# Dynamic depthwise convolution block: two taps of the upper channels made by ScalarE and GpSimd, 50 side columns, rings of x without copied rows

## Chip, core and metric

One of the eight cores of a Trainium2 chip. The metric is the device time of one execution in microseconds (us), as the median of the runs shown.

## What is computed

Two layers, each `x = x + f(gn(x))`, on x of 16 images x 128 channels x 128 x 128, in float32. `gn` is a group normalization over groups of four channels.

```python
def _L0_conv_ref(x, w_in, b_in, kg_w1, kg_b1, kg_w2, kg_b2, w_out, b_out):
    xh = _conv1x1(x, w_in, b_in)                      # 128 -> 256 channels
    pooled = jnp.mean(xh, axis=(2, 3))
    hcx = jax.nn.relu(pooled @ kg_w1.T + kg_b1)
    kernels = (hcx @ kg_w2.T + kg_b2).reshape(b, c, K, K)   # a 3x3 kernel per image and channel
    y = jax.lax.conv_general_dilated(x_r, k_r, window_strides=(1, 1), padding=((1, 1), (1, 1)),
                                     feature_group_count=b * c, ...)   # depthwise
    y = y * jnp.tanh(jax.nn.softplus(y))              # Mish
    return _conv1x1(y, w_out, b_out)                  # 256 -> 128 channels
...
x = x + _L0_conv_ref(_gn(x), ...)
x = x + _L1_conv_ref(_gn(x), ...)     # FFT over channels, two 1x1 products, inverse FFT, real part, ReLU
```

The second layer is linear in front of its ReLU, so that it is one product with a 128 x 128 matrix made at the start.

## The kernel before

**Strips and slots.** An image is 16 strips of 8 rows (1024 positions a channel), the batch N = 256 strips. Channels lie on the 128 partitions. Each engine runs its own `slot(n)` once for every strip n; semaphores alone tie the engines together. In slot n the depthwise convolution of strip n is made, x of strip n+2 is cast and multiplied by w_in, the output product of strip n-1 is made, and the second layer of strip n-19 (LAG1), since it needs the statistics of a whole image.

**Who makes the depthwise convolution.** The lower 128 of the 256 channels of the first product are made by TensorE: taps and w_in are multiplied into nine 128 x 128 matrices per image (`tap_matrices` on VectorE, `taps_high` on ScalarE, `taps_low` on GpSimd), and `conv(n, t, taps)` runs, for each half strip t and each of the nine taps, three half-precision matmuls (high part of weights and x, high and low, low and high) of 4 rows x 88 columns into psA. The leftmost SIDE = 40 columns of these channels don't go there: `product_side` makes the first product for 41 columns, ScalarE puts it into `side` (`evacuate_side`), makes tap 0 from it into PSUM (`first_tap_side`), and VectorE adds taps 1 to 8 (`side_tap`, into accS). The upper 128 channels are made wholly on this way: `product_b` into psB, one bank for both halves, `evacuate(n, t)` into `xh`, tap 0 by `first_tap_b` into accB, taps 1 to 8 by VectorE's `tap`. So VectorE makes eight taps of 1024 elements and eight of 320 per strip.

**Behind it.** ScalarE applies Mish to the three results (`mish_conv`, `mish_side`, `mish_taps`). `product_out(n, t)` multiplies by w_out into psO, again one bank for both halves, and VectorE's `residual(n, t)` adds it to x in X and sums it. `layer1` multiplies x of strip n-19 into psL, `relu` on ScalarE puts it into zt, `add` on GpSimd adds it to x, and SyncE stores.

**Rings.** `hi` and `lo` hold the high and low half-precision parts of x, four strips and two more rows (RING + 2) of 130 columns: the rows at either end of the ring are copies of the rows at its other end, or zero at the border of an image, made by ScalarE's `edge_row` and in GpSimd's `cast`. `xh` and `side` are rings of the same kind. X holds 24 strips of x; SyncE loads strip n+4 in slot n once strip n-20 is stored.

**What sets the order.** Every engine works through its slot as written, and a wait holds back all that stands behind it. Besides the strip's work, the slots of an image carry small work at strips 1 and 2 (statistics of layer 1 for the image before) and 11 to 15 (statistics, kernels and tap matrices of the next image). In strips 2 and 12 `stats_rstd` takes a logarithm and an exponential, each with its own activation table, and the next Mish loads its own again.

## Time and profile before

| | us |
|---|---|
| median of 3 runs | 4215.98 (4215.41 to 4216.52) |
| the profiled execution | 4214.95 |
| its span | 4213.2 |
| TensorE matmuls busy | 4105.5 (97%) |
| VectorE busy | 3971.9 (94%) |
| ScalarE busy | 3080.4 (73%) |
| GpSimd busy | 1345.4 (32%) |
| granted TensorE clock, mean | 0.996 of 2.4 GHz |

The span is the time from the first to the last instruction of the profiled execution. Busy time is what an engine's instructions cover; matmuls and ScalarE's and VectorE's instructions overlap their neighbours a little, so that their spacing, from start to start, is shorter than their duration. A number in square brackets in a timeline is the idle time of the engine before the row, and the arrow names what ended it. Over 4000 of the 4213 us are the 256 slots; some 69 us stand before the first tap of VectorE, and some 50 us behind the last slot, for the second layer of the last image.

### The profile page before, as it was taken

The page shows a single profiled execution, that of the slowest core. Times are in us where ns is not written, and L with a number is a line of the kernel's source. Part 1 is how long each engine was busy: PE and PEld are TensorE (multiplying, and loading weights), DVE is VectorE, ACT ScalarE, POOL GpSimd, SP SyncE. Part 2 cuts the span into 40 slices and gives each one's busy share as a digit, 9 for nine tenths or more (in the row PEclk, how much of TensorE's full clock was granted, in tenths as well). Part 3 has the DMA queues.
Part 4 walks back from the last instruction along what each step waited for, and adds up shares of the span by engine and source line. Part 5 has one row for each costly group of instructions (what it writes and reads, how often), then busy time and mean ns, then how long its engine had stood idle before and what let it go on. Part 6 is the DMA issues. An engine that isn't in the chain of part 4 may idle for free.

```text
span 4213.2 us, 61339 instructions
## 1 busy us (share of the span) xinstructions
PE 4105.5 (97%) x21484; PEld 2214.4 (53%) x21484; DVE 3971.9 (94%) x5228; ACT 3080.4 (73%) x5443; POOL 1345.4 (32%) x1428
## 2 busy tenths in 40 slices
PE   5999999999999999999999999999999999999998
PEld 3455555555555555555555555555555555555553
DVE  6999999999999999999999999999999999999996
ACT  4767777777777777777777777777777777776654
POOL 1112333333333333333333323333233333333332
PEclk9999999999999999999999999999999999999999
DMA  3112223222222322222222222222222222222112
GB/s 137 51 61 76 101 95 105 94 103 96 100 101 95 105 96 100 100 96 101 97 99 100 96 102 99 100 101 96 100 99 97 101 99 103 96 100 76 61 65 115
DMA packets 111264, 401.59 MB, mean 95 GB/s; under 512 B 13232, under 2 KB 14320, under 8 KB 110704
## 3 DMA queue, kind: packets, MB, share of 16 engines
q1 hardware_dynamic: 110960, 397.67, 27.1%
q8 instruction: 174, 2.85, 0.3%
q14 instruction: 130, 1.06, 0.1%
HBM read 263.40 MB, written 134.22 MB: 94 GB/s over the span
## 4 chain that ended last, share of the span: by engine, by line
PE 82%; DVE 11%; ACT 3%; issue 2%; POOL 1%; SPq 0%; DMA 0%; ACTq 0%; DVEq 0%; POOLq 0%
PE psBO L704 18%; PE psA L657 15%; PE psA L658 14%; PE psA L659 14%; PE psL L713 9%; DVE accB L895 6%; DVE accS L906 3%; PE psBO L682 2%; PE psBO L684 2%; PE psBO L683 2%; PE psA L667 1%; DVE X L916 1%; POOL lo L1071 1%; PE psBO L693 1%; PE psBO L695 1%
## 5 line engine op out<-in xcount | busy, mean ns | idle before, releaser
L895 DVE SCALAR_TENSOR_TENSOR accB<-xh,vectors,accB 128x1024 f32<-128x1024 f32 x2048 | 2633.2, 1286 | 67.1 <-ACT accB L414 38.0
L657 PE MATMUL psA<-hi,wa 128*128 128x352 f16 x4608 | 1450.6, 315 | 0.8 <-issue 0.8
L658 PE MATMUL psA<-lo,wa 128*128 128x352 f16 x4608 | 1442.5, 313 | 0.0
L659 PE MATMUL psA<-hi,wa 128*128 128x352 f16 x4608 | 1442.0, 313 | 0.0
L1076 POOL TENSOR_TENSOR X<-X,zt 128x512 f32<-128x512 f32 x480 | 609.1, 1269 | 1791.4 <-ACT zt L472 1789.9
L906 DVE SCALAR_TENSOR_TENSOR accS<-side,vectors,accS 128x320 f32<-128x320 f32 x2048 | 1130.8, 552 | 26.2
L704 PE MATMUL psBO<-wm,woutt 128*128 128x512 f32 x2048 | 967.0, 595 | 34.1 <-DVE X L916 31.3
L704 PEld LDWEIGHTS psBO<-wm,woutt 128*128 128x128 f32 x2048 | 384.8, 190 | 520.2 <-issue 519.1
L658 PEld LDWEIGHTS psA<-lo,wa 128*128 128x128 f16 x4608 | 443.8, 96 | 333.4 <-issue 85.2
L657 PEld LDWEIGHTS psA<-hi,wa 128*128 128x128 f16 x4608 | 442.7, 96 | 327.1 <-issue 70.5
L396 ACT ACTIVATE xh<-psBO,vectors 128x512 f32<-128x512 f32 x510 | 350.0, 686 | 359.5 <-PE psBO L684 359.4
L1071 POOL TENSOR_TENSOR lo<-X,hi 128x1024 f16<-128x1024 f32 x256 | 529.4, 2068 | 236.3 <-ACT hi L381 236.2
L659 PEld LDWEIGHTS psA<-hi,wa 128*128 128x128 f16 x4608 | 440.6, 96 | 260.4
L713 PE MATMUL psL<-X,lpt 128*128 128x512 f32 x960 | 489.6, 591 | 2.3 <-ACT zt L472 2.3
L431 ACT ACTIVATE wm<-psA,vectors 128x352 f32<-128x352 f32 x512 | 277.5, 542 | 261.8 <-PE psA L659 261.4
L916 DVE SCALAR_TENSOR_TENSOR X<-psBO,vectors,X 128x512 f32<-128x512 f32 x512 | 382.7, 747 | 52.1 <-PE psBO L704 40.8
L472 ACT ACTIVATE zt<-psL,vectors 128x512 f32<-128x512 f32 x480 | 327.0, 681 | 49.2 <-PE psL L713 49.2
L414 ACT ACTIVATE accB<-xh,vectors 128x1024 f32<-128x1024 f32 x256 | 286.2, 1118 | 29.7 <-ACT wm L443 0.8
L443 ACT ACTIVATE wm<-accB 128x1024 f32<-128x1024 f32 x256 | 261.1, 1020 | 44.0 <-DVE accB L895 43.2
L381 ACT ACTIVATE hi<-X 128x1024 f16<-128x1024 f32 x256 | 268.2, 1048 | 0.0
L463 ACT ACTIVATE junk<-X 128x1024 f16<-128x1024 f32 x256 | 267.0, 1043 | 0.3 <-DVE X L916 0.2
L456 ACT ACTIVATE junk<-XS 128x1024 f16<-128x1024 f32 x240 | 252.0, 1050 | 0.0
(173 smaller groups left out, 3192.7 us busy)
## 6 DMA issues: line engine op xcount, KB each, us to landing
X<-in_x_dram SPq DMA_DIRECT2D x256, 512.0 KB, 3.3
out_dram<-X SPq DMA_DIRECT2D x256, 512.0 KB, 2.6
XS<-in_x_dram SPq DMA_DIRECT2D x240, 512.0 KB, 3.3
X<-in_w_t_dram SPq DMA_DIRECT2D x2, 1152.0 KB, 17.6
w1t<-in_w_t_dram SPq DMA_DIRECT2D x1, 256.0 KB, 2.8
wint<-in_w_in_t_dram SPq DMA_DIRECT2D x1, 128.0 KB, 2.2
woutt<-in_w_out_t_dram SPq DMA_DIRECT2D x1, 128.0 KB, 2.7
valid<-in_valid_m_dram SPq DMA_DIRECT2D x1, 66.0 KB, 2.2
```

The lines of the kernel that those rows point to most:

```text
L396: act(xh[:, r0:r0 + 4, 1:1 + W], ps, ACT.Identity, bias=b1).then_inc(s_xe, 1)
L472: act(zt[:, t, :], psL[:], ACT.Relu, bias=lb[:, i % 2:i % 2 + 1]).then_inc(s_re, 1)
L657: mm(o, wh, xhi, start=(tap == 0), stop=False)
L658: mm(o, wh, xlo, start=False, stop=False)
L659: last = mm(o, wl, xhi, start=False, stop=(tap == TAPS - 1))
L704: last = mm(psO, woutt[:, h, :], wm[:, n % 2, h, t * TP:(t + 1) * TP], start=(h == 0), stop=(h == 1))
L713: mm(psL[:], lpt[:, i % 2, :], half(m, t), start=True, stop=True).then_inc(s_lm, 1)
L895: V.scalar_tensor_tensor(out=acc, in0=xh[:, 8 * j + dy:8 * j + dy + 8, dx:dx + W], scalar=kk[i % 2][:, TAPS + k:TAPS + k + 1], in1=acc, op ...
L906: V.scalar_tensor_tensor(out=side_out(), in0=side[:, 8 * j + dy:8 * j + dy + 8, dx:dx + SIDE], scalar=kk[i % 2][:, k:k + 1], in1=side_out( ...
L916: V.scalar_tensor_tensor(out=half(n, t), in0=psO, scalar=boutp[:, 0:1], in1=half(n, t), op0=ALU.add, op1=ALU.add, accum_out=sum1[:, k:k + ...
L1071: P.tensor_tensor(lo[:, 8 * j + 1:8 * j + 9, 1:1 + W], xs, hi[:, 8 * j + 1:8 * j + 9, 1:1 + W], ALU.subtract).then_inc(s_lo, 1)
L1076: P.tensor_tensor(half(m, t), half(m, t), zt[:, t, :], ALU.add).then_inc(s_add, 1)
```

## The change

Constants: SIDE goes from 40 to 50 (the convolution's matmuls get 78 columns a row, the side taps 50, the side product 51), XS_SLOTS from 24 to 23, with x loaded three strips ahead. EXTRA = 1 is the number of taps that ScalarE and GpSimd add to the first one, NB = 7 the number left to VectorE.

**Taps of the upper channels.** Taps 0 and 1 of strip n+1 are made by ScalarE as two products in float32 into two SBUF tiles, `tsum` and `tprod`, in slot n in front of `mish_conv(n, 0)`. GpSimd adds `tprod` to `tsum` (`tap_add`). VectorE's first tap, tap 2, reads `xh` and `tsum` and writes accB; taps 3 to 8 go on as before. `first_tap_b` behind `mish_taps` is gone. GpSimd's slot n starts with a wait for that first tap of strip n. On VectorE every tap is now followed by another accumulator's work, and `residual(n-1, 0)` stands behind side tap 7.

**Rings.** `hi` and `lo` have 32 rows of 128 columns and nothing copied. `conv` begins with tap 4 (the middle), which covers the whole output; rows beyond the image are left out, taps of the right column take 77 columns, and a matmul whose rows wrap round the ring's end is cut in two (`pieces`).

**Scratch.** The sums of squares go into `tprod` or over XS itself, as float32, where `junk` was half precision; the first `XS` sum must be complete before the squares.

```diff
-XS_SLOTS = 24
+XS_SLOTS = 23
-SIDE = 40
+SIDE = 50
+EXTRA = 1
+NB = TAPS - 1 - EXTRA
...
-        hi = sb("hi", [C, RING + 2, PW], F16)
-        lo = sb("lo", [C, RING + 2, PW], F16)
+        hi = sb("hi", [C, RING, W], F16)
+        lo = sb("lo", [C, RING, W], F16)
...
-        junk = sb("junk", [C, 3, SP], F16)
+        tsum = sb("tsum", [C, SP])
+        tprod = sb("tprod", [C, SP])
...
-            def first_tap_b(n):
+            def tap_product(n, k):
+
                 i, j = n // STRIPS, n % 4
-                eng.wait_ge(s_xe, min(3 * n + (6 if n == 0 else 5), 3 * N))
+                eng.wait_ge(s_xe, 3 * n + 2)
                 eng.wait_ge(s_kk, i + 1)
-                if n >= 1:
-                    eng.wait_ge(s_wB, n)
-                act(rows_of(accB[:]), xh[:, 8 * j:8 * j + 8, 0:W], ACT.Copy,
-                    scale=kk[i % 2][:, TAPS:TAPS + 1]).then_inc(s_kb0, 1)
+                if k == 0:
+                    if n >= 1:
+                        eng.wait_ge(s_tap, NB * (n - 1) + 1)
+                    dst, done = tsum, s_t0
+                else:
+                    if k >= 2:
+                        eng.wait_ge(s_ta, EXTRA * n + k - 1)
+                    elif n >= 3:
+                        eng.wait_ge(s_b1, n - 2)
+                    dst, done = tprod, s_t1
+                act(rows_of(dst[:]), xh[:, 8 * j:8 * j + 8, k:k + W], ACT.Copy,
+                    scale=kk[i % 2][:, TAPS + k:TAPS + k + 1]).then_inc(done, 1)
...
-                act(junk[:, 0, :], XS[:], ACT.Copy, accum_out=sumx[:, c % STRIPS:c % STRIPS + 1]).then_inc(s_sx, 1)
+                act(XS[:], XS[:], ACT.Copy, accum_out=sumx[:, c % STRIPS:c % STRIPS + 1]).then_inc(s_sx, 1)
...
             def squares_1(n):
                 s = n % STRIPS
                 eng.wait_ge(s_x1, 2 * n + 2)
-                if n >= 1:
+                eng.wait_ge(s_ta, EXTRA * min(n + 3, N))
+                if n >= N - 2:
                     eng.wait_ge(s_b1, n)
-                act(junk[:, 2, :], strip(n), ACT.Square, accum_out=sq1[:, s:s + 1]).then_inc(s_b1, 1)
+                act(tprod[:], strip(n), ACT.Square, accum_out=sq1[:, s:s + 1]).then_inc(s_b1, 1)
...
+            ORDER = (4, 0, 1, 2, 3, 5, 6, 7, 8)
+
+            def pieces(n, t, dy):
+
+                s, j = n % STRIPS, n % 4
+                rows = [r for r in range(4) if 0 <= 8 * s + 4 * t + r + dy - 1 < H]
+                at = [(8 * j + 4 * t + r + dy - 1) % RING for r in rows]
+                cut = [q for q in range(1, len(rows)) if at[q] != at[q - 1] + 1]
+                ends = [0] + cut + [len(rows)]
+                return [(rows[a], at[a], e - a) for a, e in zip(ends, ends[1:])]
+
...
+                    cols = CW - (dx == 2)
...
+                    for w, src in ((wh, hi), (wh, lo), (wl, hi)):
+                        todo = pieces(n, t, dy)
+                        for r, at, q in todo:
+                            last = mm(o[:, r:r + q, 0:cols], w, src[:, at:at + q, SIDE + dx - 1:SIDE + dx - 1 + cols],
...
+            def tap(n, q):
+
+                i, j, k = n // STRIPS, n % 4, EXTRA + q
+                if q == 1:
+                    eng.wait_ge(s_ta, EXTRA * (n + 1))
+                    if n >= 1:
+                        eng.wait_ge(s_wB, n)
...
+                                       in1=rows_of((tsum if q == 1 else accB)[:]),
...
+            def tap_add(n, k):
+                eng.wait_ge(s_t0, n + 1)
+                eng.wait_ge(s_t1, EXTRA * n + k)
...
+                P.tensor_tensor(tsum[:], tsum[:], tprod[:], ALU.add).then_inc(s_ta, 1)
...
             def slot(n):
                 b, s, m = n // STRIPS, n % STRIPS, n - LAG1
+
+                eng.wait_ge(s_tap, NB * n + 1)
                 if m >= 1:
                     add(m - 1, 1)
```

Line numbers shift: in the changed kernel L929 is the tap, L941 the side tap, L951 the residual, L425 the product of a tap, L442 the Mish of psA, L483 the ReLU of psL, L398 the evacuation of psB into xh, L474 the squares of x after the first layer, L462 and L466 the sum and squares of the next image's x.

VectorE where one strip's slot ends and the next begins, before (the first three rows are the end of slot n-1, L895 opens slot n):

```order
L906 SCALAR_TENSOR_TENSOR accS<-side,vectors,accS 128x320 x2
L916 SCALAR_TENSOR_TENSOR X,vectors<-psBO,vectors,X 128x512
L906 SCALAR_TENSOR_TENSOR accS<-side,vectors,accS 128x320 x3
L895 SCALAR_TENSOR_TENSOR accB<-xh,vectors,accB 128x1024
L916 SCALAR_TENSOR_TENSOR X,vectors<-psBO,vectors,X 128x512
L895 SCALAR_TENSOR_TENSOR accB<-xh,vectors,accB 128x1024 x4
```

The same place now:

```order
L929 SCALAR_TENSOR_TENSOR accB<-xh,vectors,accB 128x1024
L941 SCALAR_TENSOR_TENSOR accS<-side,vectors,accS 128x400
L951 SCALAR_TENSOR_TENSOR X,vectors<-psBO,vectors,X 128x512
L941 SCALAR_TENSOR_TENSOR accS<-side,vectors,accS 128x400
L929 SCALAR_TENSOR_TENSOR accB<-xh,vectors,tsum 128x1024
L951 SCALAR_TENSOR_TENSOR X,vectors<-psBO,vectors,X 128x512
```

One side tap stands behind the first residual where three stood, the tap that opens a strip reads tsum in place of accB, and no two taps of accB are neighbours.

ScalarE in strip 2 of an image, from the ReLU of psL to the evacuation of psB, before (L319 and L321 are the logarithm and the exponential of `stats_rstd`):

```order
L472 ACTIVATE zt<-psL,vectors 128x512
L437 ACTIVATE wm<-accS 128x8x40
L423 ACTIVATE accS<-side,vectors 128x320
L431 ACTIVATE wm<-psA,vectors 128x4x88
L366 ACTIVATE hi<-X 128x128
L381 ACTIVATE hi<-X 128x8x128
L319 ACT_TABLE_LOAD
...
L463 ACTIVATE junk,vectors<-X 128x1024
L431 ACT_TABLE_LOAD
...
L451 ACTIVATE junk,vectors<-XS 128x1024
...
L396 ACTIVATE xh<-psBO,vectors 128x4x128
```

and now:

```order
L448 ACTIVATE wm<-accS 128x8x50
L434 ACTIVATE accS<-side,vectors 128x400
...
L383 ACTIVATE hi<-X 128x1024
L325 ACT_TABLE_LOAD
...
L474 ACTIVATE tprod,vectors<-X 128x1024
L425 ACTIVATE tsum<-xh,vectors 128x1024
L425 ACTIVATE tprod<-xh,vectors 128x1024
L442 ACT_TABLE_LOAD
...
L462 ACTIVATE XS,vectors<-XS 128x1024
...
L398 ACTIVATE xh<-psBO,vectors 128x4x128
```

The two products stand between the squares and the Mish of psA, so in front of the evacuation; the copied row of `hi` is gone.

## Rows read from the trace of the kernel before

**Rows 1.** Windows: stretch, length; busy of PE, PEld, DVE, ACT, POOL; clock, DMA.
```profile
160.29:252.35 92.06, 84.48 (x442) 44.97 (x441) 90.78 (x121) 62.61 (x111) 14.19 (x12) 1.00 0.12 41
2012.79:2028.32 15.53, 15.53 (x79) 8.24 (x77) 15.22 (x21) 11.92 (x26) 5.26 (x5) 1.00 0.30 102
```
**Rows 2.** Costliest groups: busy us, mean ns of one | idle before.
```profile
L895 DVE SCALAR_TENSOR_TENSOR accB<-xh,vectors,accB 128x1024 f32<-128x1024 f32 x2048 | 2633.2, 1286 | 67.1 <-ACT accB L414 38.0
...
L1076 POOL TENSOR_TENSOR X<-X,zt 128x512 f32<-128x512 f32 x480 | 609.1, 1269 | 1791.4 <-ACT zt L472 1789.9
...
L658 PEld LDWEIGHTS psA<-lo,wa 128*128 128x128 f16 x4608 | 443.8, 96 | 333.4 <-issue 85.2
...
L1071 POOL TENSOR_TENSOR lo<-X,hi 128x1024 f16<-128x1024 f32 x256 | 529.4, 2068 | 236.3 <-ACT hi L381 236.2
...
L381 ACT ACTIVATE hi<-X 128x1024 f16<-128x1024 f32 x256 | 268.2, 1048 | 0.0
```
**Rows 3.** Timeline of TensorE, second half of a strip: start us, length us.
```profile
2007.31 0.38 PE L682 MATMUL psBO<-hi,wb 128*128 128x512 f16 x1
...
2007.96 0.31 PE L657 MATMUL psA<-hi,wa 128*128 128x352 f16 x1
...
2009.78 0.31 PE L693 MATMUL psBO<-hi,wb 128*128 128x328 f16 x1
...
2010.21 1.02 PE L713 MATMUL psL<-X,lpt 128*128 128x512 f32 x2
2011.07 1.88 PE L704 MATMUL psBO<-wm,woutt 128*128 128x512 f32 x4
2012.79 0.32 PE L657 MATMUL psA<-hi,wa 128*128 128x352 f16 x1
```
**Rows 4.** Timeline of TensorE, small matmuls of strip 13, each with its weight load.
```profile
2070.74 0.16 PE L624 MATMUL psA<-hv,w2p 128*128 128x2 f16 x1
...
2072.49 0.16 PE L624 MATMUL psA<-hv,w2p 128*128 128x2 f16 x1
```
**Rows 5.** Timeline of VectorE, taps, side taps and residuals.
```profile
2003.30 0.55 DVE L906 SCALAR_TENSOR_TENSOR accS<-side,vectors,accS 128x320 f32<-128x320 f32 x1
2003.75 1.28 DVE L895 SCALAR_TENSOR_TENSOR accB<-xh,vectors,accB 128x1024 f32<-128x1024 f32 x1
2004.95 0.55 DVE L906 SCALAR_TENSOR_TENSOR accS<-side,vectors,accS 128x320 f32<-128x320 f32 x1
...
2012.99 0.75 DVE L916 SCALAR_TENSOR_TENSOR X<-psBO,vectors,X 128x512 f32<-128x512 f32 x1
...
2013.66 5.26 DVE L895 SCALAR_TENSOR_TENSOR accB<-xh,vectors,accB 128x1024 f32<-128x1024 f32 x4
```
**Rows 6.** Timeline of ScalarE: a first tap; ReLU to evacuation in strip 12.
```profile
2010.13 1.12 ACT L414 ACTIVATE accB<-xh,vectors 128x1024 f32<-128x1024 f32 x1
2011.19 0.28 ACT L368 ACTIVATE side<-psBO,vectors 128x41 f32<-128x41 f32 x1
...
2042.55 0.68 ACT L472 ACTIVATE zt<-psL,vectors 128x512 f32<-128x512 f32 x1
...
2045.64 1.28 ACT L319 ACT_TABLE_LOAD   x1
...
2053.06 0.69 ACT L396 ACTIVATE xh<-psBO,vectors 128x512 f32<-128x512 f32 x1
```
**Rows 7.** Timelines: where TensorE waited in strip 15 and in strip 2.
```profile
2110.90 0.08 DVE L916 DVE_READ_ACCUMULATOR X<-psBO,vectors,X 128x1 f32 x1
...
2111.12 1.96 PE L704 MATMUL psBO<-wm,woutt 128*128 128x512 f32 x4 [0.98 <-DVE X L916]
...
2154.32 0.28 PE L643 MATMUL psA<-vectors,lt 128*128 128x1 f32 x2
2154.98 0.39 PE L682 MATMUL psBO<-hi,wb 128*128 128x512 f16 x1 [0.38 <-ACT xh L396]
```
**Rows 8.** One line of VectorE at the end: duration ns min/median/max.
```profile
L981 DVE TENSOR_TENSOR X<-X,wm x16: 1224/1226/1226, 4182.7 to 4208.7; 128x1024 f32<-128x1024 f32 x16
```

150 lines of the change are left out of this document (73 added, 77 removed).

## The prediction

> **What bounds the kernel now.** I read the windows of time first, then the costliest groups, then the timelines of TensorE, VectorE and ScalarE over single strips. A strip is eight image rows, one turn of the main loop; its time 0 is here its first convolution matmul. Taps are counted from 0. In an ordinary strip of the middle TensorE is busy 15.53 of 15.53 us and VectorE 15.22 [rows 1]: TensorE is the bound, VectorE 2% behind it. TensorE's sequence can be laid out from starts [rows 3]: 352-column matmuls come every 0.152 us (2007.96 to 2009.78, twelve of them), 512-column ones every 0.217, 328-column ones every 0.143, the layer-1 product takes 0.86, half an output product 1.72. 54 convolution matmuls, six 512s, three 328s, two layer-1 and two output products give 15.1; two small bias matmuls with their change of shape are the rest, 0.2 each. In the first 18 strips there is no layer 1, TensorE has 1.72 us less to do, and yet a strip takes 92.06/6 = 15.34 us with VectorE at 90.78 of 92.06 [rows 1]: that is VectorE's own floor. So a gain needs both engines to get lighter, and ScalarE and GpSimd, busy 11.9 and 5.3 of 15.5 us [rows 1], must take it.
>
> **TensorE's part.** A convolution matmul falls from 352 to 312 columns (308 for the three taps of the right column). The step from 352 to 512 is 0.065 us for 160 columns, 0.00041 us a column, so 312 columns come every 0.135. 54 x 0.0164 + 18 x 4 x 0.00041 = 0.92 us off a strip. The side product grows from 328 to 408 columns: 3 x 80 x 0.00041 = 0.10 on. Without copied rows a matmul whose rows wrap round the ring is cut in two: 864 more in all. Each has its own weight load and little to stream; 71 matmuls of 2 columns with a load each follow at 0.025 us (1.75 over 70 [rows 4]), so the cut itself costs the fixed part of a matmul, 0.009 us by the same line: 0.03 a strip. Were the weight load's 0.096 us [rows 2] exposed each time it would be 83 us in all; rows 4 show it is not, and I take 8. A strip's TensorE time becomes 15.53 - 0.92 + 0.10 + 0.03 = **14.75 us**, 0.775 less. Laid out: convolution of the first half to 3.8, layer 1 to 4.7, output product to 6.4, product into psB to 7.1, five taps of the second half to 9.3, psB again to 9.9, four taps to 11.6, side product to 12.1, layer 1 to 12.9, output product to the end. Scaling from the 328-column spacing instead gives 0.137 each and 0.09 us a strip more (+21 us in all).
>
> **VectorE's part.** A tap between two others of another accumulator costs its spacing, 1.19 us; a side tap 0.46 [rows 5], and 80 elements more of it 0.08 (1286 - 552 ns over 704 elements [rows 2, 5]), so 0.54; a residual 0.67. Four taps in a row took 5.26, 1.31 each, since each waits for the one before. Now there are 7 taps, all with a side tap or residual between: 7 x 1.19 + 8 x 0.54 + 2 x 0.67 = **14.0 us**, 0.75 under TensorE. From a residual at 0.2 it ends tap 8 at 11.4 and the strip at 13.0, does tap 2 of the next strip and waits 0.75 for the next residual. `mish_taps` (1.02) after tap 8 frees accB at 12.5. Tap 2 reads two SBUF tensors. The nearest row, an addition with both in SBUF, takes 1226 ns [rows 8] against 1286 [rows 2]: no dearer. It stands just before that wait, so 0.75 us covers a surprise.
>
> Here a rule speaks against the change. 2048 taps with one SBUF input average 1286 ns [rows 2] beside a GpSimd that works a third of the time, as they do in single rows: nobody is held. No row has a two-SBUF operation of VectorE beside GpSimd. The Trainium skill, page "SBUF — State Buffer", section "Who interferes with whom", says that a VectorE instruction with two SBUF inputs and a GpSimd instruction that reads SBUF exclude each other for their whole length. By the rows alone tap 2 costs 1.29 always; by the rule it could also wait for a whole GpSimd addition (rival 4); no run here shows that yet.
>
> In this order it can hardly happen: GpSimd's turn now begins with a wait for that very tap, and its work ends near 8.3 us of a strip, while tap 2 runs just before the next strip's start. Only in the last strip of an image can a GpSimd piece of 0.9 us meet it.
>
> **ScalarE's part.** Off: the first tap into PSUM (spacing 1.06, 2010.13 to 2011.19 [rows 6]), the copied rows of `hi`. On: two products into SBUF. The nearest spacings are 0.1 under the durations 1048 (32-bit to 16-bit in SBUF [rows 2]) and 1.12 (the tap into PSUM): 0.95 to 1.06, and I take 1.06, that of the same operation; side work 0.08 more for each of three. The wait that matters: `evacuate(n+2, 0)` must empty psB before TensorE's next product. ScalarE's run-up to it starts at a ReLU of psL, which waits for layer 1's product: in the new strip it ends at 12.93 after time 0, visible to ScalarE 0.2 later, so that the ReLU starts 1.6 us before the next time 0. Work from there to the evacuation, in spacings: ReLU 0.57, side Mish 0.64, side tap 0.55, Mish 0.39, cast 0.95, squares 1.05, two products 2.12, Mish 0.40, ReLU 0.57, sum 1.05 = 8.3, so it is ready at 6.6; TensorE's data come at 7.2 and psB is needed at 9.3. Ordinary strips have 1.9 us of margin and nothing waits.
>
> GpSimd gets one addition of 1024 elements: between 2.07 and 2 x 1.27 us [rows 2] for 1024 elements of two inputs and twice 512, from about 4.6 to 7.1 of a strip, needed at 13. Hidden. X in 23 slots with loads three strips ahead: the cast needs its strip some 8 us after the load can have landed. Hidden.
>
> **Where ScalarE is late.** In strips 2 and 12 of an image it loads tables three times (1.28 us each, one in rows 6). In strip 124 from the ReLU (2042.55) to the evacuation (2053.06) is 10.51 us. Now 2.12 for products, 0.17 for side work, less 0.08 for the smaller Mish: 12.72, from -1.6: the evacuation starts at 11.1 and ends at 11.8. TensorE wants psB at 9.3 + 0.3 for small products of the kind in [rows 7]: it stands **2.2 us**. In strip 2 it stood 0.38 already [rows 7], and by the same steps will stand 2.5: **2.1 more**. Such a stall isn't given back, for TensorE is the bound; ScalarE catches up within the strip, since TensorE's delay puts its own next waits off too. In strip 15 VectorE's extra matrices made TensorE wait 0.98 for a residual [rows 7]; the new order puts that residual later, the matrix wait is shorter, and I get 1.25, so 0.3 more, and 0.1 in strip 14.
>
> **The residual's place.** `residual(n-1, 0)` moves behind seven side taps and has only side tap 8 and tap 2 behind it. TensorE's output product waits for it, and the next residual for that product. This circle is 12.3 from the start of the one residual to the end of the other, 0.22 for its readout and signal (2110.90 to 2111.12 [rows 7]), 1.8 for the product when it had to wait, and 0.2: 14.5 us. It is under 14.75 by 0.25, so it does not bind in the middle, but it sets the first 18 strips, where TensorE needs only 13.0: 15.34 becomes 14.5.
>
> **The sum**, against the profiled execution (4214.95 us, of which the span is 4213.2; the median of three is 1.0 higher): 237 strips with layer 1 x -0.775 = -183.7. Table strips: 14 x 2.1 + 14 x 2.25 = +60.9. Strips 14 and 15 of 14 images: 14 x 0.4 = +5.6. The first 18: 13 ordinary ones x -0.84, the rest -2.6: -13.5. Before the very first tap of VectorE now come a second product and an addition, 1.06 + 2.4: +3.5. The clearing of `hi` and `lo` at the start lay under the loading of x: 0. The last strips: -1. Together -128: 4214.95 - 128 = 4087, as a median **4088 us**.
>
> **Rivals.** (1) *The small margins bind in every strip.* The residual's circle has 0.25 us, tap 2 behind `mish_taps` 0.5. If the spacing of a tap pair with 400 elements is 0.07 over my 1.73, the circle is 14.95. 0.2 to 0.4 a strip over 237 gives 4135 to 4183. For it: VectorE's and TensorE's floors are near each other already. Against: spacings repeat to 0.01 us. (2) *The table strips cost little*, if the two products go at 0.95 and ScalarE gets ahead: without the 61 us, 4027; half of it, 4057. Against: strip 2 waits today. (3) *The cut of columns does not do what it says*: 328 columns come at 0.143 where the line gives 0.142. If that is a floor for smaller ones, a strip is 15.2 and the time 4190. Against: rows 4. (4) *The port*: tap 2 held in every strip by a GpSimd addition of up to 2.5 us, 0.75 of it covered: 4088 + 237 x 1.75 = about 4500; it needs GpSimd to be at work at the strip's end, which its wait excludes. (5) *Slower than before: ScalarE becomes the bound.* Four of its operations before the evacuation (squares, two products, sum) now write 32-bit values to SBUF from SBUF, which no row shows; the nearest write 16-bit values (1048 ns [rows 2]) or PSUM (1.12 us [rows 6]). The margin is 1.9 us a strip and the remaining gain 0.5: from 0.6 us longer for each of the four the kernel is slower than before. At double length it is 4.2 - 1.9 = 2.3 a strip, about 4640. Against: all ScalarE rows follow elements, whatever they write.
>
> **How the numbers follow.** The forecast (4060 to 4120) 0.67; (1) 0.12; (2) 0.09; (3) 0.04; (4) 0.02; (5) 0.03; something not seen 0.03. Sizes unknown within the forecast: column spacing +21, products -6 to +3, start and first strips 5 either way. 4050 to 4150 holds the forecast, half of (1) and half of (2). A measurement can tell about 0.2% from no change. Faster by more: the first three, (3), and little else: 0.91. Same 0.02. Slower: (4), (5) and part of the unseen: 0.07.
>
> **What would show it.** Ordinary strips every 14.75 us with TensorE without a gap; convolution matmuls every 0.135; cut ones at 0.04 and 0.10; residual waits of 0.7 on VectorE; TensorE's first product into psB waiting for ScalarE once in strips 2 and 12, for 2 to 2.5 us, and nowhere else; tap 2 at 1.29 us. Wrong would be: waits of TensorE in ordinary strips, for a residual (rival 1) or for an evacuation (5).

## The result and the profile after

| | before | after |
|---|---|---|
| median | 4216.25 us (4215.41 to 4216.85, 4 runs) | 4100.68 us (4099.94 to 4105.0, 4 runs) |
| ratio | | 0.9728, interval 0.9711 to 0.9745 |
| span of the profiled execution | 4213.2 | 4103.2 |
| mean granted clock | 0.996 | 0.989 |
| TensorE, VectorE busy | 97%, 94% | 95%, 90% |
| ScalarE, GpSimd busy | 73%, 32% | 81%, 47% |

The forecast was 4088 us, 4050 to 4150. The time is 116 us shorter, and the span 110 us where the sum said 128.

The windows of the changed kernel, beside [rows 1] of before: a stretch among the first strips (87.06 us, six times 14.51; it opens in the slower strip 5), an ordinary strip, and strips 2 and 12 of an image (a strip 12 in which the clock fell). Columns: stretch, length; busy of PE, PEld, DVE, ACT, POOL; clock, DMA.
```profile
160.29:247.35 87.06, 78.59 (x446) 45.20 (x445) 83.69 (x115) 67.50 (x112) 27.01 (x12) 0.98 0.13 37
2142.19:2156.82 14.63, 14.63 (x78) 8.39 (x77) 14.12 (x19) 12.55 (x22) 6.97 (x5) 1.00 0.33 109
...
2095.32:2112.86 17.54, 15.19 (x80) 8.61 (x79) 14.22 (x19) 16.92 (x28) 9.20 (x13) 1.00 0.27 91
...
749.07:768.01 18.94, 17.10 (x92) 9.79 (x90) 14.21 (x19) 16.37 (x26) 9.84 (x15) 0.91 0.25 84
```
TensorE fills an ordinary strip, now 14.63 us where it was 15.53; VectorE has 14.12 of work in it, ScalarE 12.55. In strip 2 TensorE works 15.19 of 17.54 us while ScalarE is busy 16.92: there it is ScalarE that everything waits for.

The costliest groups of the page after, for comparison with [rows 2] (busy us, mean ns of one | idle before, releaser):
```profile
L929 DVE SCALAR_TENSOR_TENSOR accB<-xh,vectors,accB 128x1024 f32<-128x1024 f32 x1536 | 1970.2, 1283 | 0.0
...
L732 PE MATMUL psBO<-wm,woutt 128*128 128x512 f32 x2048 | 970.9, 596 | 67.7 <-DVE X L951 66.3
L1095 POOL TENSOR_TENSOR lo<-X,hi 128x1024 f16<-128x1024 f32 x256 | 546.9, 2136 | 452.3 <-ACT hi L383 444.0
L1103 POOL TENSOR_TENSOR tsum<-tsum,tprod 128x1024 f32<-128x1024 f32 x256 | 604.7, 2362 | 266.1 <-ACT tprod L425 266.1
...
L951 DVE SCALAR_TENSOR_TENSOR X<-psBO,vectors,X 128x512 f32<-128x512 f32 x512 | 383.0, 748 | 200.3 <-PE psBO L732 200.3
...
L929 DVE SCALAR_TENSOR_TENSOR accB<-xh,vectors,tsum 128x1024 f32<-128x1024 f32 x256 | 329.7, 1288 | 78.7 <-issue 70.0
...
L425 ACT ACTIVATE tsum<-xh,vectors 128x1024 f32<-128x1024 f32 x256 | 291.6, 1139 | 3.0 <-DVE accB L929 2.5
...
L474 ACT ACTIVATE tprod<-X 128x1024 f32<-128x1024 f32 x256 | 267.5, 1045 | 2.9 <-DVE X L951 2.7
```
The tap with both inputs in SBUF (L929 from tsum) takes 1288 ns against 1283 for its neighbours. ScalarE's products take 1.14 us and come 1.04 apart, the squares into tprod 1.05: writing 32-bit values costs nothing more (1048 ns in [rows 2] for 16-bit ones).

Where TensorE waited: the timeline of TensorE at strip 12, at the end of strips 14 and 15, and in strip 2, to be read beside [rows 7].
```profile
2008.51 0.39 PE L710 MATMUL psBO<-hi,wb 128*128 128x512 f16 x1 [1.59 <-ACT xh L398]
...
2046.62 1.96 PE L732 MATMUL psBO<-wm,woutt 128*128 128x512 f32 x4 [1.29 <-DVE X L951]
...
2064.25 0.67 PE L732 MATMUL psBO<-wm,woutt 128*128 128x512 f32 x1 [1.56 <-DVE X L951]
...
2107.50 0.39 PE L710 MATMUL psBO<-hi,wb 128*128 128x512 f16 x1 [2.08 <-ACT xh L398]
```

Taking each strip's start from TensorE's first convolution matmul, the 110 us are made up so (strip numbers within an image; the rows with a count of 14 hold those behind the first 18 strips):

| strips | change each, us | in all | the sum had |
|---|---|---|---|
| 166 ordinary | -0.906 | -150.4 | -128.6 |
| 14 x strip 2 | +1.62 | +22.6 | +18.6 |
| 14 x strip 12 | +2.03 | +28.4 | +20.7 |
| 14 x strip 13 | -0.9 | -12.6 | -10.9 |
| 14 x strip 14 | +0.63 | +8.8 | -9.5 |
| 14 x strip 15 | -0.60 | -8.5 | -6.7 |
| the first ones, from strip 2 of image 0 to strip 2 of image 1 | | -2.0 | -13.5 |
| start (until strip 2 begins) and end | | +3.6 | +2.5 |

### The profile page after: what moved, and what is told of

It reads as the page before. It is cut to its first block, busy times and chain, and to the rows that moved or that the text cites. A ratio compares the mean times of both kernels' runs of the same rounds, so it can differ in the third digit from the quotient of the medians.

```text
span 4103.2 us, 64873 instructions
## 1 busy us (share of the span) xinstructions
PE 3904.4 (95%) x22348; PEld 2284.5 (56%) x22348; DVE 3698.1 (90%) x4970; ACT 3331.4 (81%) x5571; POOL 1929.0 (47%) x1556
## 3 DMA queue, kind: packets, MB, share of 16 engines
q14 instruction: 144, 1.18, 0.1%
## 4 chain that ended last, share of the span: by engine, by line
PE 79%; DVE 10%; ACT 6%; issue 4%; POOL 0%; SPq 0%; DMA 0%; ACTq 0%; POOLq 0%; DVEq 0%
PE psA L686 38%; PE psBO L732 20%; PE psL L741 9%; DVE accB L929 5%; DVE accS L941 3%; PE psBO L710 2%; PE psBO L712 2%; PE psBO L711 2%; DVE X L951 1%; PE psA L695 1%; ACT L442 1%; PE psBO L721 1%; PE psBO L723 1%; PE psBO L722 1%; ACT tprod L425 1%
## 5 line engine op out<-in xcount | busy, mean ns | idle before, releaser
L686 PE MATMUL psA<-hi,wa 128*128 128x312 f16 (+4 forms) x9792 | 2078.6, 291 | 0.8 <-DVE wtmp L911 0.8
L929 DVE SCALAR_TENSOR_TENSOR accB<-xh,vectors,accB 128x1024 f32<-128x1024 f32 x1536 | 1970.2, 1283 | 0.0
L686 PE MATMUL psA<-lo,wa 128*128 128x312 f16 (+5 forms) x4896 | 1375.3, 291 | 0.0
L941 DVE SCALAR_TENSOR_TENSOR accS<-side,vectors,accS 128x400 f32<-128x400 f32 x2048 | 1296.5, 633 | 5.3 <-ACT accS L434 5.2
L1107 POOL TENSOR_TENSOR X<-X,zt 128x512 f32<-128x512 f32 x480 | 609.6, 1270 | 1181.8 <-DVE accB L929 996.3
L1103 POOL TENSOR_TENSOR tsum<-tsum,tprod 128x1024 f32<-128x1024 f32 x256 | 604.7, 2362 | 266.1 <-ACT tprod L425 266.1
L951 DVE SCALAR_TENSOR_TENSOR X<-psBO,vectors,X 128x512 f32<-128x512 f32 x512 | 383.0, 748 | 200.3 <-PE psBO L732 200.3
L398 ACT ACTIVATE xh<-psBO,vectors 128x512 f32<-128x512 f32 x510 | 351.2, 689 | 202.6 <-PE psBO L712 202.3
L929 DVE SCALAR_TENSOR_TENSOR accB<-xh,vectors,tsum 128x1024 f32<-128x1024 f32 x256 | 329.7, 1288 | 78.7 <-issue 70.0
L483 ACT ACTIVATE zt<-psL,vectors 128x512 f32<-128x512 f32 x480 | 327.7, 683 | 30.2 <-PE psL L741 26.9
L425 ACT ACTIVATE tsum<-xh,vectors 128x1024 f32<-128x1024 f32 x256 | 291.6, 1139 | 3.0 <-DVE accB L929 2.5
L425 ACT ACTIVATE tprod<-xh,vectors 128x1024 f32<-128x1024 f32 x256 | 291.3, 1138 | 0.0
L474 ACT ACTIVATE tprod<-X 128x1024 f32<-128x1024 f32 x256 | 267.5, 1045 | 2.9 <-DVE X L951 2.7
L383 ACT ACTIVATE hi<-X 128x1024 f16<-128x1024 f32 x256 | 267.7, 1046 | 0.5
L442 ACT ACTIVATE wm<-psA,vectors 128x312 f32<-128x312 f32 x512 | 258.8, 505 | 2.8 <-PE psA L686 2.4
```

The costliest lines, as they stand in the source:

```text
L398: act(xh[:, r0:r0 + 4, 1:1 + W], ps, ACT.Identity, bias=b1).then_inc(s_xe, 1)
L425: act(rows_of(dst[:]), xh[:, 8 * j:8 * j + 8, k:k + W], ACT.Copy, scale=kk[i % 2][:, TAPS + k:TAPS + k + 1]).then_inc(done, 1)
L483: act(zt[:, t, :], psL[:], ACT.Relu, bias=lb[:, i % 2:i % 2 + 1]).then_inc(s_re, 1)
L686: last = mm(o[:, r:r + q, 0:cols], w, src[:, at:at + q, SIDE + dx - 1:SIDE + dx - 1 + cols], start=(tap == ORDER[0] and w is wh and src is ...
L929: V.scalar_tensor_tensor(out=rows_of(accB[:]), in0=xh[:, 8 * j + dy:8 * j + dy + 8, dx:dx + W], scalar=kk[i % 2][:, TAPS + k:TAPS + k + 1] ...
L941: V.scalar_tensor_tensor(out=side_out(), in0=side[:, 8 * j + dy:8 * j + dy + 8, dx:dx + SIDE], scalar=kk[i % 2][:, k:k + 1], in1=side_out( ...
```

## The experiments

The theory I went in with: the ordinary strips are bound by TensorE alone, VectorE's relief is what lets the cut columns count, and all that is lost is lost in strips 2, 12, 14 and 15, through the order in which ScalarE and VectorE do their small work. The rivals: a total that is reached (ScalarE's or VectorE's), a granted clock that falls of its own, the shared port.

### Each half of the change alone

`e3_before_side50`: the kernel before, with 50 side columns.
```diff
-XS_SLOTS = 24
+XS_SLOTS = 23
...
-SIDE = 40
+SIDE = 50
...
-                if STRIPS <= n + 4 < N:
-                    load_x(n + 4)
+                if STRIPS <= n + 3 < N:
+                    load_x(n + 3)
```


> The kernel before with 50 side columns and nothing else but 23 places for X with loads three strips ahead (it would not fit otherwise): TensorE gets the whole cut of columns, VectorE keeps its eight taps. Theory (VectorE's floor of 15.34 us a strip is right behind TensorE's 15.53 in the kernel before, so the columns alone turn the bound over): VectorE's floor becomes 15.34 + 8 x 0.08 = 16.0 us, every strip takes about that, 255 x 0.46 = about 118 us longer, 4334 us, with TensorE busy about 92%. Rival (the floor of the early strips is their own, and in the middle TensorE alone decides): 14.7 us a strip and about 4010 us.

Measured: 4303.7 us, 2.1% slower than before (ratio 1.0207, 1.0186 to 1.0227). An ordinary strip's window, and its end on TensorE:
```profile
2024.75:2040.75 16.00, 14.97 (x78) 8.19 (x77) 15.79 (x21) 11.42 (x18) 4.62 (x4) 1.00 0.30 98
...
2038.96 1.96 PE L704 MATMUL psBO<-wm,woutt 128*128 128x512 f32 x4 [1.03 <-DVE X L916]
```
Ordinary strips take 16.01 us, VectorE fills 15.79 of them and TensorE waits 1.03 for the residual. The columns alone turn the bound over, and the rival (14.7 us a strip) falls. The time came out 30 us under the expectation, which had every strip 0.46 us longer: strips 13 and 14 became 0.6 us shorter than before and strips 0, 1 and 3 came to 15.4 to 15.8 on average, and that outweighs strip 15, which grew by 1.9.

`e4_after_side40`: the changed kernel with 40 side columns, so the two offloaded taps and the rings alone.
```diff
-SIDE = 50
+SIDE = 40
```


> The changed kernel with 40 side columns as before: the two taps made by products and an addition, and the rings without copied rows, alone. Theory (TensorE bounds, and has 0.03 us more to do for the cut matmuls): ordinary strips 15.56 us, the first 18 about 1 us shorter than in the kernel before, strips 2 and 12 still stand for the evacuation, 1 to 1.5 us: 4215 + 7 + 30 - 17 + 4 = about 4239 us, 4220 to 4255. Rival (lighter VectorE gives time by itself, since TensorE waits for it in many strips of the kernel before): 4180 us or less.

Measured: 4245.73 us (ratio 1.0069, 1.0049 to 1.009): slower than before by 0.7%, as the main expectation said. An ordinary strip:
```profile
2007.37:2022.81 15.44, 15.44 (x79) 8.35 (x78) 13.55 (x19) 12.55 (x22) 7.02 (x5) 1.00 0.31 102
```
VectorE has 13.55 us of work and it gains nothing, for TensorE has 15.44. So neither half is a gain: one costs 87 us, the other 30, and both together give 116. It also splits the ordinary strip's 0.90: from 15.44 to 14.63 by the ten columns is 0.81 (the sum had 0.79 to 0.82 for columns and side product), and from 15.53 to 15.44 by the rings and the shorter right-hand taps is 0.09, where the sum had about nothing. TensorE's groups of matmuls are each up to 0.04 us shorter there. The shorter right-hand taps are 0.03 of it by the sum; what gives the rest is not shown, since this run changes rings and taps together.

### ScalarE in strips 2 and 12

`e1_defer`:
```diff
+                late = (s == 12 and b < B - 1) or (s == 2 and b >= 1)
-                if n >= 2:
+                if n >= 2 and not late:
                     squares_1(n - 2)
...
+                if late:
+                    evacuate(n + 2, 0)
                 for c in stats[0:1]:
                     sum_x(c)
-                if n + 2 < N:
+                if n + 2 < N and not late:
                     evacuate(n + 2, 0)
...
+                if late:
+                    squares_1(n - 2, True)
```


> The changed kernel with ScalarE's order altered in the strips 2 and 12 of an image only: the squares of strip n-2 (1.05 us) go to the strip's end, and the sum of a strip of the next image (1.05 us) goes behind the evacuation into xh. The two products stay where they are. Theory (ScalarE is late there by what it does before the evacuation): the evacuation comes 2.1 us earlier, TensorE's waits for it (1.6 us in strip 12, 2.1 us in strip 2, changed kernel) go to 0 and about 0.2 us, and with them the halved clock that follows the stall in about half of these strips (1.65 us each in 10 of 28). Strip 12 falls from 18.1 us on average to about 15.5, strip 2 from 17.8 to about 15.2; 28 x 2.6 = 75 us less, about 4026 us. Rival A (ScalarE's whole load of those strips is too much, so the lateness only moves into strips 3 and 13): those get 1 us or more longer and the gain is under 35 us. Rival B (the halved clock comes of its own, not from the stalls): the waits go, some spells of halved clock stay, about 4050 us.

Measured: 4050.01 us (ratio 0.9605, 0.9591 to 0.9619), so 51 us less than the changed kernel. The windows of a strip 12, a strip 2 and the strip 3 behind it, and the only wait left in that strip 12:
```profile
1970.31:1986.09 15.78, 15.34 (x91) 9.10 (x90) 14.22 (x19) 15.66 (x25) 9.09 (x15) 1.00 0.30 100
2067.54:2083.68 16.14, 15.10 (x81) 8.56 (x80) 14.21 (x19) 16.02 (x27) 8.45 (x12) 1.00 0.30 98
2083.68:2098.50 14.82, 14.82 (x88) 8.63 (x87) 14.20 (x19) 12.79 (x22) 7.13 (x5) 1.00 0.34 108
...
1982.98 0.35 PE L727 MATMUL psBO<-hi,wb 128*128 128x408 f16 x1 [0.43 <-ACT xh L398]
```
The stall for the first evacuation is gone in strip 12, 0.52 us of it is left in strip 2, and no stretch at half clock is left in the middle of the kernel. Rival A falls (strip 3 got 0.16 longer, 13 stayed). Rival B falls by the trace alone, for the time is just the 4050 that it had named: its stretches of halved clock are absent. The gain is 24 us short of the 75 expected because the sum and squares that went behind the first evacuation stand in front of the second one, for which TensorE now waits 0.43 us in strip 12 and 0.52 in strip 2, and because of the 0.52 left for the first one in strip 2, where 0.2 was expected.

`e7_one_more` loads ScalarE instead: the Mish behind the products starts 1.18 us later in an ordinary strip (5.87 us into it, not 4.69).
```diff
-                act(rows_of(dst[:]), xh[:, 8 * j:8 * j + 8, k:k + W], ACT.Copy,
-                    scale=kk[i % 2][:, TAPS + k:TAPS + k + 1]).then_inc(done, 1)
+                for r in range(2 - k):
+                    if r == 1:
+                        eng.wait_ge(s_t0, 2 * n + 1)
+                    act(rows_of(dst[:]), xh[:, 8 * j:8 * j + 8, k:k + W], ACT.Copy,
+                        scale=kk[i % 2][:, TAPS + k:TAPS + k + 1]).then_inc(done, 1)
...
-                eng.wait_ge(s_t0, n + 1)
+                eng.wait_ge(s_t0, 2 * n + 2)
```


> The changed kernel with the first product of each strip (tsum, tap 0) made twice by ScalarE: 1.13 to 1.25 us more work for ScalarE in front of the evacuation of every strip, nothing else. Theory (ordinary strips have a margin of 1.9 us before that evacuation and strips 2 and 12 none): ordinary strips stay at 14.63 to 14.66 us; strips 2 and 12 get 1.1 to 1.3 us longer each, 28 x 1.2 = 34, and some more of them have the halved clock, about 4145 us. Rival (ScalarE is close to the bound everywhere, at 81% busy): ordinary strips longer by 0.3 us or more, above 4180 us.

Measured: 4196.74 us (4187.89 to 4196.89). A strip 12, an ordinary strip, and the two waits in that strip 12:
```profile
2036.22:2057.47 21.25, 18.25 (x91) 10.30 (x90) 14.22 (x19) 17.60 (x27) 9.83 (x15) 0.84 0.23 74
2189.57:2204.21 14.64, 14.64 (x78) 8.39 (x77) 14.12 (x19) 13.57 (x23) 6.98 (x5) 1.00 0.35 109
...
2047.10 0.61 PE L625 MATMUL psA<-vectors,wint 128*128 128x2 f32 x4 [1.41 <-ACT wm L445]
2049.30 0.61 PE L713 MATMUL psBO<-hi,wb 128*128 128x512 f16 x1 [1.59 <-ACT xh L398]
```
The time alone would have pointed to the rival. The strips say otherwise: ordinary ones are 14.63 to 14.66 us as before, with 13.57 of ScalarE in them, so ScalarE's margin is at least 1.1 us there. Of the 96 us, 86 are in strips 2 and 12. The wait of TensorE grew by 1.17 us there (for a Mish that frees the bank of the small products, 1.41 where it was 0.24), and the clock now fell in 27 of the 28, in 24 of them for twice as long (6.8 us in place of 3.4): strip 12 averages 21.0 us against 17.9.

### The halved clock

The rows of a strip 12 of the changed kernel in which it fell (columns as above), then TensorE's timeline there, and in the last two rows behind the wait at the end of strip 15:
```profile
749.07:761.20 12.13, 10.29 (x68) 6.36 (x67) 11.92 (x16) 12.04 (x18) 8.81 (x12) 1.00 0.25 87
761.20:765.00 3.80, 3.80 (x16) 2.10 (x15) 2.29 (x4) 2.33 (x5) 0.35 (x2) 0.56 0.46 140
...
760.99 0.39 PE L710 MATMUL psBO<-hi,wb 128*128 128x512 f16 x1 [1.59 <-ACT xh L398]
...
761.65 0.46 PE L686 MATMUL psA<-hi,wa 128*128 128x308 f16 x1
761.91 0.46 PE L686 MATMUL psA<-lo,wa 128*128 128x308 f16 x1
...
2066.04 0.30 PE L686 MATMUL psA<-hi,wa 128*128 128x312 f16 x1
2066.17 0.30 PE L686 MATMUL psA<-lo,wa 128*128 128x312 f16 x1
```
After a wait of 1.59 us TensorE worked at 1.2 GHz for 3.4 us: convolution matmuls of 308 columns come 0.26 us apart, not 0.13. Such a strip is 1.4 to 1.7 us longer than the same strip of an image in which the clock stays up. In the profiled execution it happened in 9 of the 28 strips 2 and 12 of the table, 14 us of the 51 that these strips cost (a tenth, the strip 2 of image 1, stands among the first ones; the 10 of 28 in an expectation above counts it in). In `e2_matrices` below, with the same waits, it happened in 17 of the 28.

The stalls bring it about: it left the middle of the kernel with them in `e1_defer` and in `e9_plan` and `e11_plan52` below, and came in 27 of 28 strips with the 1.41 and 1.59 of `e7_one_more`. But the length of one wait doesn't decide it. The last two rows stand behind the 1.56 us at the end of strip 15 (2064.25 above), and there TensorE goes on at full clock, matmuls of 312 columns 0.13 apart, as it does in all 14 strips 15; so it does behind the 1.59 us in strip 15 of `e1_defer`. Behind the 2.73 us in strip 15 of `e3_before_side50` it fell in 11 of 14. Strips 2 and 12 differ from 15 in that a shorter wait and the small products stand just ahead of the long wait; that this is the reason is not shown.

This goes with the scatter of the runs. The four runs of `e2_matrices` took 4060.48, 4073.37, 4081.91 and 4088.64 us at mean granted clocks of 0.992, 0.989, 0.986 and 0.984, while the four runs of each kernel without it in the middle agree to about 2 us.

### VectorE's order in strips 14 and 15

`e2_matrices`:
```diff
-                if s == 14 and build:
-                    tap_matrices(b + 1, 0, small_bank(0))
-                if s == 15 and build:
-                    tap_matrices(b + 1, 2, small_bank(0))
                 tap(n, 6)
                 side_tap(n, 6)
                 tap(n, 7)
                 side_tap(n, 7)
                 if n >= 1:
                     residual(n - 1, 0)
+                if s == 14 and build:
+                    tap_matrices(b + 1, 0, small_bank(0))
+                if s == 15 and build:
+                    tap_matrices(b + 1, 2, small_bank(0))
                 side_tap(n, 8)
```


> The changed kernel with VectorE's tap matrices of the next image (number 0 in strip 14, number 2 in strip 15) placed behind residual(n-1, 0), with side tap 8 and tap 2 of the next strip behind them, and not behind side tap 5. Theory (VectorE stands 2.2 us in front of the matrix for TensorE's small products, and the residual behind it comes late to TensorE's output product): VectorE's wait there is under 0.2 us, TensorE's wait for the residual in strip 14 goes from 1.29 us to 0 to 0.2, in strip 15 from 1.56 to about 0.5 (VectorE's own work in it is 15.1 us). 14 x (1.2 + 1.0) = 31 us less, about 4070 us. Rival (what TensorE waits for is only moved: the bank it may enter at the next strip's start waits for the same matrices): TensorE waits at the start of strips 15 and 0 and the time stays within 8 us of 4101.

What it undoes, in the timeline of VectorE in strip 14: the kernel before, where the matrices came without a wait, and the changed kernel, where they wait 2.23 us for TensorE's small products (the last of these starts at 2041.42), and the residual behind them starts at 2045.73, 0.9 us before TensorE's product that waits for it (2046.62 above).
```profile
2089.47 0.55 DVE L883 TENSOR_TENSOR wtmp<-psA,wn 128x384 f32<-128x384 f32 x1
...
2041.79 0.56 DVE L911 TENSOR_TENSOR wtmp<-psA,wn 128x384 f32<-128x384 f32 x1 [2.23 <-issue]
...
2045.73 0.74 DVE L951 SCALAR_TENSOR_TENSOR X<-psBO,vectors,X 128x512 f32<-128x512 f32 x1
```
Measured: 4077.64 us (4060.48 to 4088.64; ratio 0.9662, 0.9632 to 0.9693). Strip 14 went from 17.30 to 15.77 us without a wait, strip 15 from 17.62 to 16.70 with 0.67 us left: 34 us, near the 31 expected. The profiled execution shows only 23 us of it, because the clock fell in 17 and not 9 of the 28 strips 2 and 12. No new wait stood at the start of strips 15 and 0, so the rival falls.

### The circle of the residuals

`e6_residual` moves residual(n-1, 0) in front of tap 8:
```diff
+                if n >= 1:
+                    residual(n - 1, 0)
                 tap(n, 7)
                 side_tap(n, 7)
-                if n >= 1:
-                    residual(n - 1, 0)
                 side_tap(n, 8)
```


> The changed kernel with residual(n-1, 0) in front of tap 8 (q = 7) and side tap 7, not behind them: 1.73 us earlier in each strip; side taps 7 and 8 then follow each other. Theory (the circle of residual, output product, next residual sets the first 18 strips at 14.51 us, and makes strips 14 and 15 late): the first strips fall to VectorE's own 14.0 to 14.1 us, TensorE's waits for the residual in strips 14 (1.29) and 15 (1.56) go, ordinary strips stay at 14.64. 18 x 0.4 + 14 x 2.6 = 43 us less, about 4058. Rival (order in VectorE has no room: the two side taps in a row and tap 2, now only 1.2 us behind tap 8, wait for each other and for the Mish of accB, and VectorE becomes the bound): ordinary strips 14.8 to 15.0 us, the time above 4110.

Measured: 4171.17 us (4170.03 to 4172.31): 70 us slower than the changed kernel. Both the theory and the rival, as written, are wrong. An ordinary strip, a stretch of the early strips, and a strip 12 with its new wait:
```profile
2204.39:2219.05 14.66, 14.66 (x88) 8.72 (x87) 14.38 (x19) 12.08 (x20) 7.01 (x4) 1.00 0.34 107
163.90:249.30 85.40, 80.16 (x466) 45.67 (x467) 84.87 (x115) 66.19 (x114) 27.65 (x15) 1.00 0.13 36
2022.36:2043.22 20.86, 18.12 (x91) 10.26 (x90) 14.71 (x20) 17.27 (x28) 10.22 (x15) 0.84 0.23 75
...
2032.98 0.38 PE L622 MATMUL psA<-vectors,wint 128*128 128x2 f32 x2 [1.15 <-ACT wm L442]
```
The first strips did fall, from 14.51 to 14.24, with VectorE full (84.87 of 85.40), and ordinary ones stayed at 14.66. Strip 14 fell by 1.5 us and its wait for the residual went, as the theory said. The loss is in strips 0, 1, 15 (0.4 to 0.6 us each) and in 2 and 12 (2.8 and 2.0), where TensorE waits for an evacuation or a Mish of ScalarE: the Mish of accB can only start when tap 8 has ended, and behind it stand the evacuation of the side columns, the ReLU and the side Mish, with which ScalarE's run-up begins. Tap 8 came 0.7 us later in ordinary strips (10.82 us into the strip, not 10.09) and 1.3 later in strip 11, where a side tap also waited 0.57 us for ScalarE; the side Mish of that strip 12 began 0.03 us before TensorE's first matmul where it had been 0.93 before, and TensorE paid 1.15 us at L622 and, in 12 of 14 strips 12, the halved clock on top. In the prediction I had let that run-up start with layer 1's product; it starts with whichever comes later, and tap 8 is the nearer one.

`e10_swap` moves it less far, and leaves tap 8 where it was:
```diff
                 tap(n, 7)
+                if n >= 1:
+                    residual(n - 1, 0)
                 side_tap(n, 7)
-                if n >= 1:
-                    residual(n - 1, 0)
                 side_tap(n, 8)
```


> The changed kernel with residual(n-1, 0) in front of side tap 7 and not behind it, tap 8 staying where it is; side taps 7 and 8 then follow each other. Theory (the circle of the residuals sets the first strips at 14.51 us; the earlier run with the residual in front of tap 8 lost time because tap 8, with it the Mish of accB and all that stands behind it on ScalarE, came 0.7 us later): the first strips at 13.97 to 14.1 us if VectorE's floor takes over, TensorE's waits in strips 14 and 15 about 0.5 us shorter, strips 2 and 12 as in the changed kernel or 0.1 worse: about 4101 - 6 - 14 = 4081 us, but up to 20 us either way by how many stalls are followed by the halved clock. Rival (any later side tap 8 makes ScalarE late, since the Mish of the side columns stands at the head of its run-up): strips 2 and 12 longer by 0.5 us or more each, the time above 4101.

Measured: 4099.26 us (4098.77 to 4099.75), within 2 us of the changed kernel. A stretch of the first strips:
```profile
160.00:245.00 85.00, 78.27 (x455) 45.66 (x453) 84.78 (x116) 67.02 (x114) 27.64 (x15) 1.00 0.14 38
```
With tap 8 in its place, strips 2 and 12 waited just as in the changed kernel (0.24 and 1.59, 0.26 and 2.07), strips 14 and 15 fell by 0.54 and 0.45 us, and the first strips to 14.15 us, where VectorE is busy 84.78 of 85.00. So 14.51 was the circle, 14.15 is VectorE's own floor with two side taps in a row (the 14.0 of the sum with 0.15 for that). By the strips' lengths this is worth 19 us, and the time didn't show it, for the clock fell in 11 of the 14 strips 2 of this execution, where it had been 3. The rival falls (its waits in strips 2 and 12 are absent; a new one of 0.36 us for an evacuation stands in strip 15 alone), and the expected 4081 missed within the 20 us that I had left to the clock.

### The port

`e5_no_wait`:
```diff
-                eng.wait_ge(s_tap, NB * n + 1)
                 if m >= 1:
                     add(m - 1, 1)
```


> The changed kernel without the wait with which GpSimd starts each strip (for tap 2 of the strip). Its first addition of a strip (X + zt, 1.27 us) then runs as soon as its ReLU is done, about 13.9 us after the strip's first matmul, beside VectorE's tap 2 of the next strip, which has both inputs in SBUF (1.29 us, from about 13.0). Theory (these two exclude each other, as GpSimd's 1.61 us in place of 0.91 beside such a tap in strip 15 suggests): where they meet, the one that comes second is longer by the rest of the other. GpSimd comes second mostly, so its addition averages over 1.4 us in place of 1.27, tap 2 goes from 1.29 to at most 1.5, and the time stays within 10 us of 4101, since VectorE waits 0.6 us in each strip anyway. Rival A (they share freely and the 1.61 us had another reason): both keep their durations to 0.02 us. Rival B (VectorE is the one that is held): tap 2 at 1.9 us or more and the time at 4150 or more.

Measured: 4104.15 us (4103.74 to 4104.55), within 4 us of the changed kernel. The mean of GpSimd's addition, then an ordinary strip (GpSimd's addition beside VectorE's tap 2), then the one place where GpSimd was first:
```profile
L1107 POOL TENSOR_TENSOR X<-X,zt 128x512 f32<-128x512 f32 x480 | 660.3, 1376 | 1087.8 <-ACT zt L483 1087.8
...
2158.01 1.56 POOL L1107 TENSOR_TENSOR X<-X,zt 128x512 f32<-128x512 f32 x1 [5.37 <-ACT zt L483]
...
2157.17 1.29 DVE L929 SCALAR_TENSOR_TENSOR accB<-xh,vectors,tsum 128x1024 f32<-128x1024 f32 x1
...
72.80 3.13 DVE L929 SCALAR_TENSOR_TENSOR accB<-xh,vectors,tsum 128x1024 f32<-128x1024 f32 x1 [8.77 <-POOL tsum L1103]
...
72.72 2.12 POOL L1095 TENSOR_TENSOR lo<-X,hi 128x1024 f16<-128x1024 f32 x1
```
GpSimd's addition begins at 2158.01 while tap 2 runs to 2158.46, and takes 1.56 us and not 1.27: it gives up most of the overlap. At 72.72 GpSimd's cast was 0.08 us ahead; tap 2 took 3.13 us in place of 1.29 and ended 1.09 us behind the cast (74.84). The mean went from 1270 to 1376 ns, less than the 1.4 I had written, because part of the additions start when tap 2 is over. So the rival (4) of the prediction is a true mechanism that didn't come to bear: who comes second waits, GpSimd is nearly always second, and VectorE has 0.5 us to spare there.

By the Trainium skill, page "SBUF — State Buffer", section "Who interferes with whom", a VectorE instruction with two SBUF inputs and a GpSimd one that reads SBUF exclude each other and issue order decides who blocks. These rows agree in both directions: the second one is longer by 0.29 of the 0.45 us that the two would have shared, and by 1.84 of 2.04.

### Towards a faster kernel

`e8_reordered` puts several orders together: the squares of strip n-2 go out of strips 2 and 12 (made up three strips later), the next image's sum and squares behind the last evacuation, the matrices behind the residual, and in strip 15 the residual ahead of tap 8.
```diff
+                now = [] if late(n) else stats[0:1]
...
+                if late(n):
+                    for c in stats[0:1]:
+                        sum_x(c)
+                        squares_x(c)
+                for k in last:
+                    squares_1(k, n + 2)
...
+                if s == 15 and n >= 1:
+                    residual(n - 1, 0)
+                tap(n, 7)
```


> The changed kernel with three orders altered: in strips 2 and 12 the sum and the squares of the next image's strip go to the strip's end and the squares of strip n-2 go out of these strips altogether (made up three strips later); both matrices behind residual(n-1, 0) as in the run with the matrices moved; in strip 15 that residual in front of tap 8. Theory (the stalls of strips 2, 12, 14 and 15 are all of order): strip 2 about 15.1, strip 12 about 15.3, strip 3 14.7, strip 14 15.8, strip 15 16.1 us. From the run with the order of strips 2 and 12 alone (4050): 14 x (1.0 + 0.5 + 0.15 + 1.5 + 1.5) = 65 us less, 3980 to 3995 us. Rival (ScalarE's or VectorE's total is reached in strips 12 to 15, which also hold the small products): a new wait in strips 13 or 0 and above 4010 us.

Measured: 4028.42 us (ratio 0.9557, 0.9542 to 0.9573). TensorE's new waits, at the end of strip 0 and of strip 3:
```profile
2036.47 0.67 PE L755 MATMUL psBO<-wm,woutt 128*128 128x512 f32 x1 [0.92 <-DVE X L974]
...
2082.83 0.67 PE L755 MATMUL psBO<-wm,woutt 128*128 128x512 f32 x1 [0.90 <-DVE X L974]
```
Strips 2, 12, 14 and 15 came out at 15.50, 15.18, 15.77 and 15.80 us, near the expectation, but strip 3 rose to 15.99, strip 0 to 15.81, strip 13 to 17.73. The rival's signs came, a new wait and a time above 4010, but not its reason, a total that is reached: `e9_plan` removes these waits with the same work in other places. Work put at the end of ScalarE's strip stands ahead of the side Mish and of the first side tap, so VectorE begins late (its side tap 1 waited 1.39 us for ScalarE in that strip 3) and its residual is late.

`e9_plan` takes the work out rather than to the end. Its list of squares is empty in strips 2, 3, 12 and 13 and holds two in strips 4, 6, 14 and 0; the matrices are placed as in `e2_matrices`:
```diff
-                if n >= 2:
-                    squares_1(n - 2)
+                stats = stat_strips(n)
+                for k in squares_of(n)[0]:
+                    squares_1(k, n + 1)
+                if n >= 1 and late(n - 1):
+                    for c in stat_strips(n - 1):
+                        sum_x(c)
+                        squares_x(c)
...
                 mish_conv(n, 0)
+                if late(n):
+                    evacuate(n + 2, 0)
                 if m >= 0:
                     relu(m, 0)
```


> The changed kernel with ScalarE's work of strips 2 and 12 thinned and not merely shifted: no squares of strip n-2 in them or in the strip behind (made up in strips 4, 6, 14 and 0, always in front of the evacuation, where 1.25 us fit into the margin of 1.9), the sum and squares of the next image's strip one strip later, the evacuation ahead of the ReLU; and the two matrices of VectorE behind residual(n-1, 0). Theory (in the reordered run ScalarE gave its lateness on through side tap 1 to VectorE, so that TensorE waited 0.9 us for a residual in strips 0 and 3): strip 2 14.9 to 15.1 us, 3 14.7, 12 15.2, 13 17.3, 14 15.8, 15 16.7, 0 14.5, 6 14.7. 4028 - 14 x 2.7 = about 3990 us (3980 to 4000). Rival (ScalarE's total over strips 2 to 4 is what counts, wherever it stands): new waits of 0.5 us or more in strips 3, 4, 6 or 13, above 4015 us.

Measured: 3998.11 us (3997.5 to 3998.58; ratio 0.9482, 0.9468 to 0.9497), inside the range expected, and no wait of 0.5 us in strips 3, 4, 6 or 13, so the rival falls. Strip 2 took 14.86 us, 3 14.66, 12 15.02, 13 17.24, 15 16.70, 0 14.55, each within 0.2 us of what was expected. Strip 14 took 16.94 where 15.8 was expected, with this wait:
```profile
1988.03 0.39 PE L738 MATMUL psBO<-hi,wb 128*128 128x512 f16 x1 [0.99 <-ACT xh L412]
```

`e11_plan52` is that kernel with the residual in the place of `e10_swap` and this:
```diff
-SIDE = 50
+SIDE = 52
```


> The kernel of the run with ScalarE's work thinned, with the residual in front of side tap 7 as in the run with the two swapped, and 52 side columns. Theory (two columns take 0.16 us from TensorE and give VectorE 8 x 16 elements, 0.14 us): ordinary strips 14.48 us if VectorE (14.0 + 0.14 + 0.1 for two side taps in a row) and the circle (about 14.2) stay below. Against the run with 50 columns 200 x 0.16 = 32 us less, about 3960 us. Rival (VectorE or the circle becomes the bound): ordinary strips 14.6 us or more with TensorE waiting for residuals, no gain or a loss against it.

Measured: 3968.59 us (3968.23 to 3968.89; ratio 0.9412, 0.9397 to 0.9428), the best of all. An ordinary strip:
```profile
2069.23:2083.71 14.48, 14.48 (x79) 8.39 (x78) 14.33 (x20) 12.29 (x22) 7.01 (x4) 1.00 0.34 110
```
14.47 to 14.50 us with TensorE full and VectorE at 14.33: the two columns gave 0.16 us, as expected, and now TensorE and VectorE are about 1% apart. The time is 9 us over the expected 3960. Waits of 1.08 and 0.62 us for evacuations stand in strips 14 and 0; strip 0 became 0.5 us longer.

`e12_catch_up` moves the two made-up squares from strips 14 and 0 into strip 13:
```diff
+                for k in squares_of(n)[2]:
+                    squares_1(k, n + 2)
                 if b < B - 1:
                     if s == 11:
                         stats_group("x", b + 1, small_bank(0))
```


> The kernel of the run with 52 columns, with the two squares that strips 12 and 13 leave out made up inside strip 13, behind its evacuation and ahead of the read-out of the kernels, and not in strips 14 and 0. Theory (strip 13 holds TensorE's 72 tiny products, which give ScalarE some 2.5 us of idle time just there, while in strips 14 and 0 TensorE waited 1.08 and 0.62 us for an evacuation that the made-up square had pushed back): strip 14 falls from 16.86 to about 15.8, strip 0 from 15.11 to about 14.6, strip 13 stays at 17.1. 14 x (1.05 + 0.5) = 22 us less, about 3947 us. Rival A (strip 13 has no such room): it becomes 1 us or more longer and the time stays within 5 us of 3968. Rival B (the waits in strips 14 and 0 come from VectorE's matrices through the Mish of accB, not from the squares): they stay at 0.5 us or more.

Measured: 3971.02 us (ratio 0.9419, 0.9403 to 0.9435), no better than `e11_plan52`.
```profile
1962.45 0.36 PE L752 MATMUL psBO<-hi,wb 128*128 128x424 f16 x1 [1.44 <-ACT xh L413]
...
1964.43 1.29 DVE L960 SCALAR_TENSOR_TENSOR accB<-xh,vectors,tsum 128x1024 f32<-128x1024 f32 x1 [4.16 <-ACT wm L469]
```
Strip 14 fell to 15.61 and strip 0 to 14.62, so those waits did come from the squares (rival B falls); but strip 13 rose from 17.08 to about 18.7. What I took for idle time of ScalarE there was partly behind, not ahead of, what others wait for: the second evacuation and the Mish of accB came late, and VectorE's tap 2 stood 4.16 us. Rival A is right about the result.

## Why the prediction was right, step by step

**The bound.** TensorE at the bound with VectorE right behind [rows 1], so that both must get lighter: shown by the two halves alone, +87 and +30 us. The rest of the argument hangs on this, and it held.

**Ordinary strips**, term -0.775: measured -0.906, 22 us in all to the good. The term's own parts (-0.92, +0.10, +0.03) give -0.79, so 3 us of this are a slip in the adding. The spacing of 312 columns, estimated at 0.135, is 0.133 to 0.134 (twelve matmuls with their gaps took 1.6 us), and columns with side product gave 0.81. The cut matmuls cost what was said: the strips that hold one, two of every four, take 14.66 us and the others 14.63. Missed was most of the 0.09 that the changed kernel gives with 40 columns, where the sum had 0.03 off for the right-hand taps against 0.03 on for the cuts. Rival (3), a floor below 328 columns, is out. So is rival (1): TensorE has no gap in ordinary strips, and VectorE waits 0.52 us for a residual there, less than the 0.7 forecast but enough.

**Strips 2 and 12**, predicted waits of 2.5 and 2.2 us: measured 0.27 + 2.08 and 0.24 + 1.59. The mechanism is the one named, and taking ScalarE's work away in front of the evacuation removed it. Where the clock stayed up these strips take 17.54 and 17.29 us, 1.34 and 1.39 more than before, where the sum had 1.33 and 1.48. The strips still lost 4.0 and 7.7 us in all more than the sum had, since the clock fell after 9 of the 28 stalls, a term that was not there. Rival (2) is out.

**Strip 14** is the step that failed: 0.1 us of wait predicted, 1.29 measured. I had placed the matrices after side tap 5 at their old length and asked how late the residual behind them would be, not when their own input would come. TensorE makes it in the second half of its strip, and VectorE, faster now, reached the matrices 2.2 us earlier than that; in the kernel before it came to them at 11.45 us of the strip, just behind the last of TensorE's products. Moving them removed the wait. Strip 15, 1.25 predicted, had 1.56.

**The first 18 strips**, -13.5, gave -2.0. The circle of 14.5 us is right (14.51 measured; 14.24 and 14.15 once the residual was moved), but strips 2, 4 and 5 of the first image took 17.24, 15.47 and 16.43 us, its strip 14 took 18.55 (15.64 before), and strip 2 of the next image 17.41 (15.34 before). In the first three ScalarE takes two sums and squares a strip, and VectorE's side tap 1 waited 1.01, 0.87 and 0.87 us for `first_tap_side`; the clock fell in strips 2, 5 and 14 and in that next strip 2. No experiment took these sums away, so this cause is read from the timeline, not shown.

**The margins.** ScalarE's 1.9 us in ordinary strips: a delay of 1.18 us went into it without a trace, so rival (5) is out. Its starting point was wrong all the same: the run-up hangs on tap 8 as well as on layer 1, which cost 70 us when tap 8 came later. **The port**, rival (4): a true mechanism, with no effect in this order. **The start**, +3.5: strip 2 begins 3.6 us later; VectorE's first tap itself 2.8 (72.32 us, not 69.47).

Two misses of opposite sign, 22 us to the good and about 40 to the bad, left the sum 18 us too low.

## What to carry to other kernels

Where two engines are level, moving work off one gives nothing, and the same move paired with one that shifts the freed time back is worth more than the parts: cost each half alone before the pair. The time of a deep pipeline is lost at the few turns with extra work, and what helps there is to take work out of the turn altogether and do it where the margin is, not to push it to the turn's end, where it delays the next one. When a sum rests on how late an engine is, look for every chain that feeds its run-up, and for an operation that is moved ask first when its input comes.

## What the runs showed of the chip

- Stalls of TensorE of 1.6 to 2.1 us in strips 2 and 12 of a program that otherwise keeps it full were followed in 9 of 28 cases, 17 of 28 in another run, by 3.4 us at 1.2 GHz, 1.4 to 1.7 us lost on top; one of 1.56 us in strip 15 was followed by it in none of 14.
- A VectorE operation with both inputs in SBUF and a GpSimd one that reads SBUF wait for each other, whichever is second: 1.56 for 1.27 us, and 3.13 for 1.29 (`e5_no_wait`).
- A ScalarE operation on 1024 32-bit values a partition costs the same whether it writes 16- or 32-bit values to SBUF (1046 for the cast and 1045 ns for the squares in the changed kernel), with a scale read from SBUF 1139.
